# Two PV steps together at every second key block, instead of one at every key block

## The reference

```python
xn = _layernorm(x)
x = x + attention(xn, Wqkv, Wout) + ffn(xn, gate_w, w11, w33, w22, sw1, sw2, sw3)

# attention: 16 heads of 16 numbers, rotary tables on q and k, causal
scores = einsum('bhqd,bhkd->bhqk', q, k) * D ** -0.5     # masked above the diagonal
attn = softmax(scores, axis=-1)
out = einsum('bhqk,bhkd->bhqd', attn, v)                  # then @ Wout.T

# ffn: 32 experts, each row goes to 6 of them, and a shared expert
g, u = xf @ w11[e].T, xf @ w33[e].T
y = sum over chosen e of c[t, e] * (silu(g) * u) @ w22[e].T
```

## Time and profile before

| | us |
|---|---|
| median of 3 runs | 900.64 |
| lowest and highest | 897.58 and 901.23 |
| the profiled execution, its time | 899.4 |
| its span in the trace | 897.6 |
| POOL busy in it | 503.7 (56%) |
| PEld busy in it | 454.0 (51%) |

### The profile page before, as it was taken

How to read it: one execution, slowest core, us unless ns; L and a number is a source line. 1 busy time by engine, 2 the same in 40 slices (tenths; PEclk the granted TensorE clock), 3 DMA queues, 4 the chain that set the end, 5 groups by cost and what they waited for, 6 DMA issues and landing times.

```text
span 897.6 us, 17583 instructions
## 1 busy us (share of the span) xinstructions
PE 828.9 (92%) x5281; PEld 454.0 (51%) x5282; DVE 605.0 (67%) x1187; ACT 493.1 (55%) x1214; POOL 503.7 (56%) x651
## 2 busy tenths in 40 slices
PE   5799987788989999999999999999999999999997
PEld 2366654233343443378888888873344343433444
DVE  2577776878877788755555555557788777888322
ACT  3466543144646566644444444547676766667662
POOL 3556650399889821066667666526888888820000
PEclk9799988789999999999999999999999999999999
DMA  7015545620000041047778777784585555510011
GB/s 226 1 38 178 190 149 160 171 65 19 1 19 1 14 119 47 1 131 250 220 219 245 231 231 231 135 144 72 71 173 90 73 89 71 89 25 1 13 36 48
DMA packets 81986, 96.15 MB, mean 107 GB/s; under 512 B 13030, under 2 KB 73446, under 8 KB 81894
## 3 DMA queue, kind: packets, MB, share of 16 engines
q0 software_dynamic: 19968, 31.47, 19.6%
q1 hardware_dynamic: 45033, 46.80, 17.4%
q10 hardware_dynamic: 16896, 16.78, 5.5%
HBM read 61.11 MB, written 33.82 MB: 106 GB/s over the span
## 4 chain that ended last, share of the span: by engine, by line
PE 77%; DVE 12%; issue 4%; DMA 2%; DVEq 2%; SPq 1%; ACT 1%; POOLq 1%; POOL 1%; ACTq 0%
PE bank L1201 14%; PE bank L1184 13%; PE vector_banks L1276 12%; PE vector_banks L1160 11%; DVE mpart L958 8%; PE vector_banks L1052 6%; PE bank L1293 6%; PE vector_banks L1073 4%; PE bank L1073 3%; PE bank L1052 2%; DMA xn_all<-wexp 2%; PE vector_banks L1221 2%; PE vector_banks L1163 1%; PE bank L1187 1%; PE bank L1089 1%
## 5 line engine op out<-in xcount | busy, mean ns | idle before, releaser
L958 DVE TENSOR_REDUCE mpart<-vector_banks 128x2 f32<-128x1024 f32 (+3 forms) x320 | 330.0, 1062 | 82.1 <-PE vector_banks L1160 50.6
L716 ACT ACTIVATE probs<-bank 128x512 f32<-128x512 f32 (+3 forms) x428 | 212.3, 539 | 129.8 <-PE bank L1184 65.9
L1184 PE MATMUL bank<-turned 99*128 99x512 bf16 (+3 forms) x640 | 201.2, 353 | 7.7 <-DVE turned L980 2.2
L1160 PE MATMUL vector_banks<-turned 96*128 96x512 bf16 (+3 forms) x640 | 184.7, 358 | 13.2 <-DVE mpart L958 12.3
L589 POOL DMA_INDIRECT turned<-normed_rows,tok_i x128 | 125.3, 979 | 122.3 <-PE vector_banks L1052 89.1
L604 POOL DMA_INDIRECT res<-expert_rows,slot_i x96 | 148.8, 1550 | 41.4 <-issue 28.4
L716 ACT ACTIVATE at_first<-bank 128x512 f32<-128x512 f32 (+3 forms) x212 | 105.6, 533 | 71.8 <-PE bank L1187 39.1
L1184 PEld LDWEIGHTS bank<-turned 99*128 99x128 bf16 x640 | 58.3, 97 | 164.5 <-ACT probs L716 71.3
L1276 PE MATMUL vector_banks<-xn_all,probs 128*128 x512 | 135.2, 386 | 4.6 <-issue 1.6
L1201 PE MATMUL bank<-probs,V 128*32 128x512 f32 (+3 forms) x856 | 102.5, 550 | 0.0
L1276 PEld LDWEIGHTS vector_banks<-xn_all,probs 128*128 128x128 f32 x512 | 87.1, 190 | 17.4 <-issue 9.7
(11 more groups left out here) (154 smaller groups left out, 983.6 us busy)
## 6 DMA issues: line engine op xcount, KB each, us to landing
expert_rows<-probs ACTq DMA_DIRECT2D x32, 512.0 KB, 4.4
term_rows<-at_first SPq DMA_DIRECT2D x96, 128.0 KB
turned<-term_rows SPq DMA_DIRECT2D x32, 384.0 KB, 4.4
xn_all<-wexp SPq DMA_DIRECT2D x32, 384.0 KB, 4.0
normed_rows<-xn_all SPq DMA_DIRECT2D x4, 512.0 KB, 5.7
turned<-normed_rows,tok_i POOLq DMA_INDIRECT x128, 4.1
out<-res SPq DMA_DIRECT2D x16, 128.0 KB, 1.7
res<-x SPq DMA_DIRECT2D x1, 1536.0 KB, 8.9
```

The costliest lines, as they stand in the source:

```text
L716: A(PT[v // 2 % 6][:, v % 2, 0:width], bank[A_BANK[step][0]][:, 0:width], ACT.Exp).then_inc(s["scalar_bank_read"], 1)
L958: V.tensor_reduce(mpart[:, t % TPC, 2 * j:2 * j + 2, p], ring[:, :, 0:w], AX.X, ALU.max).then_inc(s["vector_bank_read"], 1)
L1160: last = mm(ring[:, h, 0:w], q_turned(slice(0, KQ), 2 * j + h, t * P, P), k_turned(par, slice(0, KQ), 2 * j + h, p * CH, w), start=True, s ...
L1184: last = mm(ring[:, 0:CH - off], k_turned(parity(g), slice(0, KM), h, kb * P, P), q_turned(slice(0, KM), h, c * CH + off, CH - off), start ...
```

## The change

When two blocks are pending, both `pv` steps are now put between the second and the third `st`, where there was one. The list is then empty, so this happens at every second key block. The number of steps of each kind is the same. The wait of ACT for the `pv` that frees a buffer was written with the number of `pv` steps ahead of it in the list; it is now written with the number of the block, and still means the `pv` of three blocks earlier.

```diff
@@ whole_order, the loop over the key blocks
         some()
         if len(pending) == 2:
             values(pending.pop(0))
+            values(pending.pop(0))
         order.append(("st", g, c, kb, 2))
@@ scalar engine, attend, the exponential of block v // HG
                         act.wait_ge(s["scalar_bank_full"], n + 1)
-                        if pvs >= 2:
-                            act.wait_ge(s["pv_done"], pvs - (h >= 2))
+                        if v // HG >= 3:
+                            act.wait_ge(s["pv_done"], v // HG - 2)
```

## The result

The changed kernel is slower: 907.87 us (median of 19 runs, 902.86 to 912.21) against 898.63 for the kernel before on the same chips (19 runs, 893.37 to 901.96). The ratio is 1.0102, with a 95% interval of 1.0085 to 1.0119, so +9.2 us. The profiled execution took 907.48 us, with a span of 905.7.

The account below looks back on a forecast made before the run. It took PE and DVE both to be near their bound. Terms of +10.1, -2.6, +4.3 and -1.9 sum to +9.9 us on 899.4, so 909.3, or 910.5 by the median; it took 909.5, range 902 to 916.

Parts of the forecast that it names:

- the wide pairs: 48 pairs of 512+512 or 512+384 columns, two `mx` a block: ring waits exceed the saving, 0.21 us each, +10.1 us.
- the dense part: Group 0, three `mx` a block, DVE the bound: nine full-width pairs each lengthen DVE's gap by 0.48 us, +4.3 us.
- the short and the free ones: 11 pairs of 256+128 columns and 8 without `mx` behind them: each only saves 0.24 us, -2.6 and -1.9 us.
- the first part: Attention before the expert stretch: claimed to end some 6 us later.
- the second: Attention after the expert stretch: claimed to take some 3 to 4 us longer.
- Rival 1: Whole kernel: no ring waits, 67 pairs save 0.24 us each, faster by 16 us to 883; chance 0.06.
- Rival 2: Whole kernel: with lower bounds, saving and ring waits cancel, -0.8 us, 899; chance 0.14.
- rival 3: Whole kernel: upper bounds of the waits give +20.7 us, 920, and clock lapses could add more; chance 0.03.
- What a pair saves, 0.24 us: On PE, two `pv` joined lose less time at the switch than two lone ones: 0.24 us a pair.
- The walk with full-width strips: Two blocks with four full-width `mx`: PE waits for rings before the third and fourth; cycle 5.99 us against 5.68.
- The lower bound of the ring waits, 0.27: Ring waits of a full-width pair if narrow strips relieve half of the cycles: 0.27 us, where 0.45 was taken.
- ACT at nothing: ACT's exponentials behind a pair: three banks, no PE wait above 0.01 us, so costed at nothing.

Follow-up runs that it names:

- half reads: DVE's row maxima read half of each score strip, against the kernel before: single `pv` 868.39 us (0.9632), with pairs 856.44 us (0.9525).
- the dense kernel: Pairs only where blocks 2 to 24 flush, one `pv` a block elsewhere, against the kernel before: 908.29 us, ratio 1.0093.

## Why the prediction was right, and where its terms were off

Direction and size were right (909.5 forecast, 907.87 measured), and so was the mechanism, but the sum was in part luck. The kernels with pairs in one part only gave 7.6 us less than forecast for the wide pairs, 4.1 more for the dense part and 5.1 more for the short and the free ones, and these errors cancel. Of the other signs, the first part grew by 4.9 us (forecast 6; by 8.9 from its first `pv` on) and the second by 2.8 (forecast 3 to 4). Rival 1, the saving wins, comes true only with short ring reads (-12 us). Rival 2, the two cancel, is nearly so for the wide pairs by themselves. Of rival 3 the clock came, and with it the upper bound in the dense part.

- *What a pair saves, 0.24 us.* Right: the second `pv` follows after 0.88 us, and splitting the pairs cost 0.22 us each.
- *The walk with full-width strips.* Right: 5.88 measured for 5.99, with ring waits at the two places named. The half reads show that these waits decide the sign.
- *The wide pairs, +10.1.* Mis-sized: alone they cost +2.5 us (interval +0.7 to +4.2), and the starts give +0.5 before the experts and +3.3 after. I had let the `mc`, `mt` and `ot` work of a chunk make up for narrow strips. It does the opposite: PE itself is held up in those cycles (7.68 us before for the pair of blocks 8 and 9 of chunk 3 in group 2, 7.00 after), and a pair fits into them. The lower bound of the ring waits, 0.27, was nearer than the 0.45 that I took: +2.5 over 48 pairs is +0.05, or 0.29 of waits.
- *The dense part, +4.3.* Mis-sized: +8.4, above its upper bound (9 x 0.88 = 7.9). The lower mean clock of that kernel (0.9680 for 0.9740) is worth 2.6 to 3.5 us of it, so 5 to 6 are left for the gaps, near the term. Its gaps of DVE came as forecast, for instance these two:

```profile
243.88 1.23 DVE L959 TENSOR_REDUCE mpart<-vector_banks 128x2 f32<-128x1024 f32 x1 [1.54 <-PE vector_banks L1161]
...
252.67 5.75 DVE L959 TENSOR_REDUCE mpart<-vector_banks 128x2 f32<-128x1024 f32 x5 [1.39 <-PE vector_banks L1161]
```

  What I missed is that a single `pv` covered PE's wait for the maxima. With it moved ahead, PE lost 0.9 us of cover and, in most such executions by the mean clocks, some us at half the clock. I had that lapse only in rival 3, as a thing of the time before 190 us. That it follows from pairs in the dense part is shown by the profiles with and without them and by the mean clocks, and that the one pair matters by the kernel without it (0.9728); why it comes in some executions of other kernels too stays open.
- *The short and the free pairs, -2.6 and -1.9.* Too large: together -0.5 us in the last chunk, and +0.6 (-1.1 to +2.4) in their own kernel. In the free part two of the seven cycles became 0.25 us shorter, as forecast; they had waits for an ACT bank before, and the same ones now. The others changed by between -0.15 and +0.24, and in four of these five PE had waited for no bank of ACT before and now does. In the one that grew (6.23 to 6.47 us) it waits for two:

```profile
880.83 1.29 PE L1185 MATMUL bank<-turned 99*128 99x512 bf16 x3
881.25 0.10 PEld L1185 LDWEIGHTS bank<-turned 99*128 99x128 bf16 x1 [0.42 <-ACT probs L717]
881.73 0.10 PEld L1185 LDWEIGHTS bank<-turned 99*128 99x128 bf16 x1 [0.39 <-ACT at_first L717]
```

- *ACT at nothing.* Right for the wide cycle shown above, which has no wait for an ACT bank, but not elsewhere: the waits for ACT's banks went from 30 to 68 over attention, and in the last chunk they take the place of the saving. With the `mx` moved to the pair they took over as the cause of waits. The wait's new form at nothing is right (0.9989, 0.9969 to 1.0009).

## What to carry to other kernels

Joining two long steps of the bound engine saves their switch once, and lets every engine that it feeds run dry for as long as the second step lasts. With two rings to run ahead, compare the time of the joined step and the first refill with what the other engine has in store; if its reads are nearly as long as the cycle, the waits afterwards are worth more than the switch. Look at every engine that it feeds: here ACT took what DVE did not. Look also at what the moved step had covered, and take such a change place by place: 20 of the 78 pairs gained 5 us, all 78 lost 9.

## What the runs showed of the hardware

Two steps of four float32 matmuls on 32 columns each, back to back, start 0.88 us apart at 512 columns, and a lone one holds up the next full-width matmul for 1.00 us. The Trainium skill (TensorEngine Tiling (Array Packing), Key Properties) names this drain at a change of mode; the runs give its size, 0.22 us a pair over 78 pairs with the lead, and 0.24 in one cycle compared directly.

The granted clock fell from 2.4 to 1.2 GHz about a wait of PE of 2.06 us, in a stretch in which PE was busy 2.46 us of 5, and in one profile about a wait of 1.17 us. In another kernel it stayed up with a wait of 1.50 us (busy 3.02 of 5). The Trainium skill (TensorE: Matmul & The Clock Gate, A second HAM failure mode: psum-queue depth-cycling) tells of a kernel whose short idles between groups of matmuls made the clock swing between its levels. The many short ring waits did not do that here: in the changed kernel's stretches from 650 to 750 us the clock was at 1.00 throughout. What these traces show is a lapse at a longer wait; the dense kernel had a further one between 250 and 265 us (mean 0.85), where PE had waited 1.14 us.

In a list of waits, the idle time of a load behind a `pv` is put down to whatever engine the load last hung on: 0.84 us each, to ACT for an `st` and to DVE for an `mx`, both of them long done. Sort such a list by what PE did before the load, or it names the wrong engine.
